# A vision tower on one core: banks of its own for the second group's embedding, the last pixel sort in pieces, tokens of four pairs together, norms in other places

## The reference, cut to what matters

```python
B, H_img = 64, 224                      # x: (64, 1, 224, 224); patches 64 x 25, stride 64 x 12
p = unfold(x)                           # (64, 51, 1600): 3 x 17 patches of 1600 pixels
h = gelu(p @ tok_weight + tok_bias)     # (64, 51, 64), erf form
h = h + attention(layernorm(h))         # 8 heads of 8
h = h + experts(layernorm(h))           # 6 experts of 3 layers, the top 2 mixed

def attention(x):
    q, k, v = split(x @ w_qkv.T + b_qkv)
    qgr, kgr = qr(q).Q, qr(k).Q                  # per image and head: 51 x 8
    dots = q @ k.T
    a = concat([dots * s0, dots**2 * s1, (qgr @ kgr.T)**2 * s2])   # 24 channels
    a = softmax(conv_w @ batchnorm(a) + conv_b)  # 24 -> 8 channels
    return (a @ v) @ w_proj.T + b_proj
```

## Time and profile before

| | |
|---|---|
| runs of the kernel | 334.08, 334.38 and 338.35 us; median 334.38 |
| the profiled execution | 336.93 us, of which the span from first to last instruction is 334.4 us |
| mean granted TensorE clock | 0.911 of full |
| TensorE matmuls busy | 283.7 us (85%) |
| VectorE busy | 201.1 us (60%) |
| ScalarE busy | 172.0 us (51%) |
| GpSimd busy | 70.5 us (21%) |

### The profile page before, as it was taken

One profiled execution on the slowest core, in us unless ns is written; L12 is line 12 of the kernel. 1 busy time (PEld: TensorE's weight loads), 2 busy tenths in 40 slices (PEclk: granted clock), 3 DMA queues, 4 the chain that ended last, 5 costly groups with the idle time before them and its releaser, 6 DMA issues.

```text
span 334.4 us, 11326 instructions
## 1 busy us (share of the span) xinstructions
PE 283.7 (85%) x4854; PEld 199.1 (60%) x4854; DVE 201.1 (60%) x549; ACT 172.0 (51%) x310; POOL 70.5 (21%) x78
## 2 busy tenths in 40 slices
PE   4296999999788578595999999999876899998883
PEld 2176766877557467474788887886755453333331
DVE  1445087967477569788465466575587362465571
ACT  2445363342523156853566885666654565445731
POOL 8001114201103131132178322352200030000000
PEclk9787999999969879789599999999999899559999
DMA  8999960000000000000000000000000000010102
GB/s 226 284 297 269 251 159 2 5 3 4 0 2 2 5 2 2 2 2 2 4 3 4 4 4 2 2 6 2 4 2 0 2 1 2 1 25 2 25 0 50
DMA packets 16848, 13.88 MB, mean 42 GB/s; under 512 B 4128, under 2 KB 16416, under 8 KB 16800
## 3 DMA queue, kind: packets, MB, share of 16 engines
q1 hardware_dynamic: 16800, 13.18, 15.9%
HBM read 12.34 MB, written 0.84 MB: 39 GB/s over the span
## 4 chain that ended last, share of the span: by engine, by line
PE 63%; DVE 17%; ACT 8%; issue 7%; SPq 2%; DMA 2%; POOL 0%; ACTq 0%; DVEq 0%; POOLq 0%
PE banks L1149 10%; PE banks L1424 8%; PE banks L1408 6%; PE banks L1435 5%; PE banks L1449 4%; PE banks L1548 3%; PE banks L1583 3%; PE banks L1532 2%; PE banks L1569 2%; PE banks L1239 2%; DMA pixels<-in_x_dram 2%; PE banks L1155 2%; DVE pixels L918 2%; PE banks L1169 1%; PE banks L1209 1%
## 5 line engine op out<-in xcount | busy, mean ns | idle before, releaser
L1424 PE MATMUL banks<-pixels,convw 64*64 64x204 f32 x768 | 43.4, 358 | 9.9 <-DVE pixels L922 9.9
L309 POOL TENSOR_TENSOR qbd<-q,weights 128x448 f32<-128x448 f32 x32 | 31.4, 984 | 89.6 <-PE banks L1408 89.4
L1149 PE MATMUL banks<-pixels,taps 64*64 64x204 f32 x800 | 40.7, 355 | 9.2 <-DVE pixels L226 6.3
L1149 PEld LDWEIGHTS banks<-pixels,taps 64*64 64x64 f32 x800 | 32.3, 142 | 15.3 <-DVE pixels L226 7.0
L918 DVE TENSOR_REDUCE pixels<-banks 128x8 f32<-128x408 f32 x32 | 18.6, 583 | 35.9 <-PE banks L1424 33.8
L1424 PEld LDWEIGHTS banks<-pixels,convw 64*64 64x64 f32 x768 | 30.1, 143 | 14.5 <-issue 11.4
L1408 PE MATMUL banks<-kbd,qbd 64*64 64x102 f32 x1024 | 33.0, 270 | 2.9 <-issue 1.5
L1408 PEld LDWEIGHTS banks<-kbd,qbd 64*64 64x64 f32 x1024 | 26.3, 144 | 7.6 <-issue 4.3
L284 POOL TENSOR_TENSOR rstd<-var_eps,minus_half 102x8 f32<-102x8 f32 x8 | 13.1, 1639 | 77.2 <-DVE var_eps L710 77.1
L523 ACT ACTIVATE pixels<-banks 128x816 f32<-128x816 f32 x32 | 27.2, 851 | 0.0
L1449 PEld LDWEIGHTS banks<-vbd,pixels 115*51 115x51 f32 x512 | 15.7, 133 | 18.1 <-issue 13.5
(11 more groups left out here) (175 smaller groups left out, 505.0 us busy)
## 6 DMA issues: line engine op xcount, KB each, us to landing
pixels<-in_x_dram SPq DMA_DIRECT2D x16, 434.0 KB, 6.8
pixels<-in_x_dram SPq DMA_DIRECT2D x32, 108.5 KB, 6.9
out_dram<-pixels SPq DMA_DIRECT2D x8, 102.0 KB
weights<-in_w_dram SPq DMA_DIRECT2D x1, 652.0 KB, 8.8
weights<-in_w_dram SPq DMA_DIRECT2D x1, 564.0 KB, 7.8
taps<-in_w_dram SPq DMA_DIRECT2D x1, 416.0 KB, 3.5
```

The source lines that it names most:

```text
L309: pool.tensor_tensor(qbd[u][:, :].rearrange("p (c h i) -> p c h i", c=QB, h=H), qv.unsqueeze(2).to_broadcast([128, QB, H, NI]), w("headmas ...
L1149: last = nc.tensor.matmul(bank[r][64 * s:64 * s + 64, 0:2 * EN], tap(u, r), src, start=(u == 0), stop=(u == PW - 1))
L1424: last = nc.tensor.matmul(bank[2 + r][64 * to:64 * to + 64, 0:4 * N], convw[64 * r:64 * r + 64, k * HI:(k + 1) * HI], src[64 * r:64 * r + ...
```

## The change

- `embed(1)` writes banks 6 and 7 (`embed_bank`), and waits for no `gelu`; `embed(2)` waits for `gelu(0)`, `embed(3)` for `gelu(2)`.
- The last sort has no part on VectorE: ScalarE does it in three pieces of 4 phases (912 elements each).
- `tokens` works on 4 pairs: 8 matmuls with the identity as the moving operand, two images' halves to partitions 0 to 50 and 64 to 114. `qk_tokens` copies 115 x 512. `gram` makes 16 matmuls into both banks 7 and 6. All three are called 8 times, not 16; `gram_blocks` 16 times, as before, each pair on one `gram`.
- `cvec` moves to bank 5 and ahead of `scale_ln(0)`; the matmuls before the first embedding have 512 columns and go to banks 4 and 5.
- `sort(6)` of VectorE comes behind the first four `gram_blocks`. TensorE's order changes: `broadcast1(1)` and `q_and_k(1)` come before `gram(1)`; eight to ten taps of `embed(2)` stand between the first half's tokens and Gram products; `broadcast1(2)` stands five taps before the end of `embed(3)`; `tokens(4)` and `gram(4)` stand around `center1(3)`, `variance1(3)` behind `tokens(5)`; `q_and_k(3)` behind `m_to_columns(0)`.
- On VectorE `variance_eps(3)` and `scale_ln(3)` leave the sign steps: the one stands behind `signed_inverse(0)`, the other behind `gram_blocks(9)`, ahead of `q_times_k(0)`; `gram_blocks(10)` comes behind `block_m(0)`.

```diff
-DVE_PHASES = (8, 8, 8, 8, 8, 8, 8, 8)
-GRAM_BANKS = [7, 6] * 8
+DVE_PHASES = (8, 8, 8, 8, 8, 8, 8, 0)
+SHARED_STEPS, ALL_SORTS = 7, 7 + 3
+GRAM_BANKS = (7, 6)
...
+        def embed_bank(g, r):
+            return bank[6 + r if g == 1 else r]
...
@@ scalar
-            def sort(e):
-                to_phases(act, act_copy, e, DVE_PHASES[e], SW, "sort_a")
+            def sort(e, part=None):
+                lo, hi = (DVE_PHASES[e], SW) if part is None else (4 * part, 4 * part + 4)
+                to_phases(act, act_copy, e, lo, hi, "sort_a")
...
-                nc.scalar.activation(qk_tok[t % 2], bank[4 + t % 2][0:N, :], ACT.Copy).then_inc(S["qk_tok_done"], 1)
+                nc.scalar.activation(qk_tok[t % 2], bank[4 + t % 2][0:64 + N, :], ACT.Copy).then_inc(S["qk_tok_done"], 1)
...
             sort(6)
+            queries(1)
+            sort(7, 0)
             qk_tokens(2)
             qk_tokens(3)
-            queries(1)
-            for t in range(4, BT):
-                qk_tokens(t)
-            sort(7)
+            sort(7, 1)
+            sort(7, 2)
...
             center(3)
-            qk_tokens(8)
-            qk_tokens(9)
-            qk_tokens(10)
-            qk_tokens(11)
+            qk_tokens(4)
+            qk_tokens(5)
             queries(3)
             keys(3)
-            qk_tokens(12)
-            qk_tokens(13)
             grass_keys(0)
-            qk_tokens(14)
-            qk_tokens(15)
+            qk_tokens(6)
+            qk_tokens(7)
@@ vector
             variance_eps(0, 3)
+            dve.wait_ge(S["cvec_mm"], 1)
+            link(nc.vector.tensor_tensor(mixc[0:HI, 15:16], bank[5][0:HI, 508:509], vec("conv_b", HI), ALU.add), "cvec")
+            link(nc.vector.tensor_copy(mixc[HI:2 * HI, 15:16], mixc[0:HI, 15:16]), "cvec")
             scale_ln(0)
             sort(5)
             keys(0)
-            dve.wait_ge(S["cvec_mm"], 1)
-            link(nc.vector.tensor_tensor(mixc[0:HI, 15:16], bank[7][0:HI, 508:509], vec("conv_b", HI), ALU.add), "cvec")
-            link(nc.vector.tensor_copy(mixc[HI:2 * HI, 15:16], mixc[0:HI, 15:16]), "cvec")
-            sort(6)
             variance_eps(1, 3)
             gram_blocks(0)
             gram_blocks(1)
             scale_ln(1)
+            keys(1)
             gram_blocks(2)
-            keys(1)
             gram_blocks(3)
-            sort(7)
+            sort(6)
...
-                elif j == 6:
-                    variance_eps(3, 3)
-                elif j == 7:
-                    scale_ln(3)
             signed_inverse(0)
+            variance_eps(3, 3)
             gram_blocks(8)
             gram_blocks(9)
+            scale_ln(3)
             q_times_k(0)
-            gram_blocks(10)
             block_m(0)
-            for t in range(11, 2 * BT):
+            for t in range(10, 2 * BT):
                 gram_blocks(t)
@@ tensor
             def q_and_k(g):
                 pe.wait_ge(S["xn_done"], g + 1)
+                if g == 0:
+                    pe.wait_ge(S["cvec"], 1)
                 if g >= 1:
-                    pe.wait_ge(S["qk_tok_done"], 4 * g)
+                    pe.wait_ge(S["qk_tok_done"], 2 * g)
...
             def tokens(t):
-                pe.wait_ge(S["q_done"], t // 4 + 1)
-                pe.wait_ge(S["k_done"], t // 4 + 1)
+                pe.wait_ge(S["q_done"], t // 2 + 1)
+                pe.wait_ge(S["k_done"], t // 2 + 1)
...
-                        last = nc.tensor.transpose(bank[4 + t % 2][0:N, (2 * a + k) * 128:(2 * a + k + 1) * 128], src[:, c], ident)
+                        for half in range(2):
+                            p = 4 * t + 2 * half + a
+                            last = nc.tensor.matmul(bank[4 + t % 2][64 * half:64 * half + N, (2 * a + k) * 128:(2 * a + k + 1) * 128],
+                                                    src[:, p * N:(p + 1) * N], ident, start=True, stop=True)
...
             def gram(t):
                 pe.wait_ge(S["qk_tok_done"], t + 1)
                 if t == 0:
-                    pe.wait_ge(S["cvec"], 2)
-                before = [i for i in range(t) if GRAM_BANKS[i] == GRAM_BANKS[t]]
-                if before:
-                    pe.wait_ge(S["gmask_done"], before[-1] + 1)
+                    pe.wait_ge(S["gelu_done"], 8)
+                if t > 0:
+                    pe.wait_ge(S["gmask_done"], 2 * t)
...
                     for half in range(2):
-                        blk = qk_tok[t % 2][:, a * 128 + 64 * half:a * 128 + 64 * half + 64]
+                        for u in range(2):
+                            blk = qk_tok[t % 2][64 * u:64 * u + N, a * 128 + 64 * half:a * 128 + 64 * half + 64]
+                            last = nc.tensor.matmul(bank[GRAM_BANKS[u]][64 * half:64 * half + 64, a * C:(a + 1) * C], blk, blk,
+                                                    start=True, stop=True)
```

More of the change, by code:

```diff
@@ L1304, in _ @@
             pe.wait_ge(S["w_embed"], 16)
-            for _ in range(4):
-                nc.tensor.matmul(bank[7][:, 0:GN], taps[:, 0:128], taps[:, 0:GN], start=True, stop=True)
+            for i in range(4):
+                nc.tensor.matmul(bank[4 + i % 2], taps[:, 0:128], taps[:, 0:512], start=True, stop=True)
             def at(f, *args):
@@ L1334, in _ @@
             gram(0)
+            broadcast1(1)
+            q_and_k(1)
+            gram(1)
+            embed(2, 0, 3)
             tokens(2)
-            gram(1)
-            broadcast1(1)
             tokens(3)
+            embed(2, 3, 5)
             gram(2)
-            q_and_k(1)
+            embed(2, 5, 8)
             gram(3)
-            embed(2, 0, 3)
-            for t in range(4, BT):
-                tokens(t)
-                if t > 4:
-                    gram(t - 1)
-            gram(BT - 1)
             first_rows(0)
-            embed(2, 3, 6)
+            embed(2, 8, 10)
             gram_rows(0)
-            embed(2, 6, 12)
+            embed(2, 10, 12)
             values_of(0)
@@ L1358, in _ @@
             variance1(2)
[L1359 removed]
+            embed(3, 8, 20)
             broadcast1(2)
+            embed(3, 20, 25)
             q_and_k(2)
+            tokens(4)
             center1(3)
[L1363 to L1364 removed]
+            gram(4)
+            tokens(5)
             variance1(3)
[L1366 to L1368 removed]
+            select_q_and_k(0)
             broadcast1(3)
[L1370 to L1372 removed]
+            m_to_columns(0)
             q_and_k(3)
[L1374 to L1377 removed]
             grass_keys(0)
[L1379 to L1384 removed]
+            gram(5)
+            tokens(6)
+            tokens(7)
+            gram(6)
+            gram(7)
             first_rows(1)
```

57 lines of the change are left out of this document (18 added, 39 removed).

## The result

| | before | after |
|---|---|---|
| median of 22 executions each | 337.5 us | 340.29 us |
| ratio after to before | | 1.0106, 95% interval 1.0055 to 1.0158 |
| profiled execution, span | 336.93, 334.4 us | 338.08, 335.9 us |
| mean granted clock in the profile | 0.911 | 0.917 |
| first `all_dots` starts | 111.48 us | 116.57 us |

The change made the kernel slower by 1.06%, 3.6 us (1.9 to 5.3). The ratio is that of the faster executions alone (8 of 22 after, 6 of 22 before, each within 1.5% of its kernel's fastest); the medians of all 22 lie 2.8 us apart. The forecast was 1.4 us slower: the direction holds, and the size is half of what the medians show and less than half of what the ratio shows.

The account below looks back on a forecast made before the run. The front before `all_dots(0)` was taken as waits, then TensorE-bound from 42.7 to 82.4 us, then an engine-to-engine chain. -4.1 + 0.3 + 5.2 gave +1.4 us: 338.3 profiled, 335.8 median; range 330.5 to 340.

Parts of the forecast that it names:

- Part 1 (banks): Second group's embedding in banks 6 and 7: no wait for `gelu(0)`, `q_and_k(0)` at 38.64 not 42.72, gain 4.1 us.
- Part 2 (calls of four): Tokens of four pairs together: `tokens` 1.0 us, `gram` 0.6 us a call, TensorE sheds 6 us.
- fourfold price: Skill's rule that fp32 transposes are four times faster than plain matmuls: 2.2 us per `tokens` call instead of 1.0.
- Part 3 (first half): First half's order: `q_and_k(1)` at 47.6, `embed(2)` ending at 66.25 not 70.04, last sort hidden; lead 3.8 us.
- The 0.3 us: Added to the sum for tokens and blocks before the second norm, turning the 4.1 us gain into 3.8.
- Part 4 (second half): Second half's order from 76.9 us: lead 3.8 us lost, +5.2 us, `all_dots(0)` at 112.9 not 111.48.
- second rival: New idle times bring the clock down before 85 us: 1.8 to 3.8 us, giving 337.6 to 339.6 us; chance 0.23.
- a sum of 1.4: Net forecast for the front: -3.8 us in the first half, +5.2 in the second, 1.4 us slower.
- three places: Second half: early `broadcast1(2)`, late last norm (1.8 us lag at `variance1(3)`), queries and six Gram blocks behind the key transform.
- Shifts one to one: Work behind `all_dots(0)`, same instructions in the same order, moves by exactly as much as `all_dots(0)` does.
- The kept lead: Rival: second half keeps the first half's lead; 330.6 us with all of it, 332.5 with half; chance 0.22.
- Tokens that don't overlap: Rival: `tokens` matmuls run one after another, 1.8 us a call, 4.8 us on the path, 340.6 us; chance 0.10.

Follow-up runs that it names:

- e4: Kernel before with only the second group's embedding in banks 6 and 7 and `cvec` in bank 5 ahead of `scale_ln(0)`: 332.07 us against 337.2, ratio 0.9814.
- e9: e1 with the last sort split between VectorE and ScalarE again, VectorE's sorts in their old places: 333.21 us against 335.97, ratio 0.9892.
- e11: e4 plus 2 unused matmuls in each of the second and fourth attention steps: 330.02 us against 335.97, ratio 0.9624.
- e1: Changed kernel with the second half of the front in the old order, still in calls of four pairs: 337.09 us against 337.57 before.
- e2: Changed kernel with only the last norm placed as before: 338.04 us against 337.57 before.
- e3: Changed kernel with 4 unused matmuls in the idle time before `m_to_columns(0)`: 338.6 us against 337.57 before.
- e5: Changed kernel with `q_and_k(3)`, `gram(5)` ahead of `m_to_columns(0)`, `tokens(6)` ahead of `grass_keys(0)`, block 10 ahead of `block_m(0)`: 339.83 us against 337.57 before.
- e10: Changed kernel with unused matmuls in all five idle times of the second half: 336.03 us against 335.97 before.
- e6b: Changed kernel with only `broadcast1(2)` behind all taps of `embed(3)` again, same program as e6, second run: 339.28 us against 335.97 before.
- e6: Changed kernel with only `broadcast1(2)` behind all 25 taps of `embed(3)` again, first run: 337.34 us against 337.2 before.

## Why the prediction was right in direction and too small

- **Part 1 (banks): right in the mechanism, and too large at its own place.** `embed(1)` no longer waits, and `q_and_k(0)` comes 2.4 (e4) to 4.4 us (e9) sooner behind the first tap, 3.5 in e11, where 4.1 was predicted. That e4 ends on -4.2 us is partly luck, as said there. The time of e4 falls, and no other part's gain is shown.
- **Part 2 (calls of four): right.** `tokens` 1.0 us, as predicted; `gram` 0.62 from start to start (107.48 to 108.10), 0.6 predicted. The fourfold price that the Trainium skill ("TensorE: Matmul & The Clock Gate", Terms) speaks of, and by which the prediction had 2.2 us a call, doesn't appear. The saved 6 us of TensorE earn nothing that these runs show: e1, which has them on top of the banks, is no faster than e4.
- **Part 3 (first half): right.** 8.7 us from `q_and_k(0)` to `q_and_k(1)`, predicted 9.0; the last sort hidden (e9). The 0.3 us are a misread row: the 1.18 us from mask to mask were the pace of the old `gram` calls, and a block that waits for nothing takes 1.0 us (47.60 - 46.60 on VectorE). So the last pair took 2.30 us too (110.75 to 113.05), not 2.45.
- **Part 4 (second half): the order right, the clock mis-sized. This is the step that failed.** The prediction saw TensorE idle 2.1 us before `broadcast1(2)` and went on with five taps of 1.8 us at the full clock. They took 3.25: the clock fell, in this profile and in every one that keeps the broadcast there unfilled (e2, e3, e5: 80 to 84.5), and with the idle times filled (e10) they took 1.92. GELU, queries and `tokens(4)` wait behind them. A low clock was the second rival, at 0.23, with this very price, 1.8 us; it belonged in the sum. Its reason against, that 1.85 us idle at 85.49 hadn't brought the clock down, was one profile's luck: the same idle time did in four of nine. The low clock was counted only for `m_to_columns` and `q_and_k(3)`; it also held for `grass_keys` (2.45 us, not 2.15) and for `first_rows(1)` with `gram_rows(1)` (1.97 us, against 1.31 in the kernel before). By the table that is 1.3 + 0.4 + 0.4 us of delay, against a sum of 1.4. The rest of the 3.7 us is the pixels' 1.9, which is chance.
- **What gives the lead back.** The prediction named three places, and each was tried: the late norm 2.6 us (e2), the Gram block and queries behind the key transform 3.5 us (e5), the early broadcast 2.6 us (e6b); all three together 6.9 (e1). They overlap, and the last two contain a part of the clock's 3.2.
- **"Shifts one to one": wrong.** `all_dots(0)` came 5.1 us later, the span 1.5. What follows is the same program, and took 215 to 226 us in the profiles (e10 215.1, e4 225.7, e11 left out). The time after the front varies by more than the change moves the front, so the 3.6 us of the ratio and the 5.1 us of the front agree only loosely, and one profile proves neither. For the profiled execution the prediction had 338.3 us, and it took 338.08. That is luck: `all_dots(0)` came 3.7 us later than predicted, and what follows took 3.6 us less than in the profile before (219.3, not 222.9).
- **The rivals.** The kept lead fell in the front. Tokens that don't overlap fell. The low clock was real: it fell for the taps, and not for `tokens(4)` to `variance1(3)`, which ran at the full clock, so the rival's lower end applies, 1.8 us above the forecast and thus 3.2 us above the kernel before. The measured 2.8 (medians) to 3.6 us (ratio) lie around that. Its price in the front, 3.2 us by e10, shares the blame with the order.
- **Open.** How much of the 3.6 us is front and how much clock elsewhere. Over 22 executions after and 45 before, 1 minus the mean clock, times the time, times two, gives 63.9 and 59.7 us at the lower level (340.2 x 2 x 0.094; 336.5 x 2 x 0.089). If all of that were work of TensorE on the path, the 4.2 us more would cost 2.1.

## What to carry to other kernels

An idle time that a reordering makes on TensorE has two prices: its own length, and what may run behind it at half the clock. In these profiles 2.14 us did it four times of four and 1.84 us four times of nine; put the second price into the sum with such a weight, and don't take one profile in which the clock held as a proof that it holds. When work is moved up behind a slower engine's result, ask which unrelated work now queues behind it: here five taps held up the last GELU. Where idle time can't be avoided, unused matmuls into a free bank can hold the clock: two of them in each of two places kept it at 1.00 from 103 to 131 us (e11), where no other profile has more than 0.88. How much time that gives isn't settled. The banks alone gained 5.1 us by the medians, while the reordering gained nothing.

## What the runs showed that was not expected

- One program, the same operations and the same waits, took 62.8 and 68.1 us for the same stretch (e6b, e6): after a fall at 86 us the clock stayed low for 24 us of plain matmuls with idle times between, though TensorE was busy 17.26 of 24 us.
- The executions of one kernel differ by 12 us and more (345.95 against 333.98 after, 343.48 against 328.92 in e5), and those with a lower mean clock are mostly the longer ones: it lies between 0.889 and 0.926 in the 22 of the changed kernel.
- The first tap, which waits for the first two steps of pixels, starts at 15.4 to 18.2 us in the profiles (e9 15.42, e4 18.15), with the same DMAs.
- In `gram_rows(1)` TensorE stopped inside a run of matmuls that wait for nothing, 2.17 us in e6b:

```profile
110.83 0.65 PE L1249 MATMUL banks<-weights,grams 128*32 128x32 f32 x30
113.65 0.74 PE L1249 MATMUL banks<-weights,grams 128*32 128x32 f32 x34 [2.17 <-issue]
```

In the changed kernel's profile the same place has no such stop, but `gram_rows(0)` has one of 0.58 us. No run here tries the cause.
